# The first norm at row 8, the second convolution in pieces, projections from row 16, another place for the rows' store and the next x

## What is computed

```python
g = (mamba(x_n) + flip(mamba(flip(x_n)))) * scale_mod      # x_n = rmsnorm(x) * w
x = x + res_scale * (g + sigmoid(dwconv3x3(x_n) + b) * x_n)
# mamba: u, z = x_n @ W_in; u = silu(conv4(u) + b); dt, B, C = u @ W_x; delta = softplus(dt @ W_dt + b)
#        h[t] = exp(delta*A) * h[t-1] + delta*u*B;  y = sum_n C*h + u*D;  out = (y * silu(z)) @ W_out
t = t + attention(layernorm(t))      # 6 heads of 64, causal, softmax in f32
t = t + gelu(layernorm(t) @ w_fc.T) @ w_proj.T   # both weights are Kronecker products
```

## Time and profile before

| what | us |
|---|---|
| median of 3 runs (4754.21 to 4781.78) | 4765.77 |
| the profiled execution | 4750.03 |
| its span, first to last instruction | 4748.2 |
| busy: VectorE | 3668.8 (77%) |
| TensorE | 3452.2 (73%) |
| GpSimd | 2577.3 (54%) |
| ScalarE | 2460.6 (52%) |

### The profile page before, as it was taken

How to read it: one execution, slowest core, us unless ns; L and a number is a source line. 1 busy time by engine, 2 the same in 40 slices (tenths; PEclk the granted TensorE clock), 3 DMA queues, 4 the chain that set the end, 5 groups by cost and what they waited for, 6 DMA issues and landing times.

```text
span 4748.2 us, 40285 instructions
## 1 busy us (share of the span) xinstructions
PE 3452.2 (73%) x11626; PEld 1752.1 (37%) x11626; DVE 3668.8 (77%) x2793; ACT 2460.6 (52%) x3459; POOL 2577.3 (54%) x1628
## 2 busy tenths in 40 slices
PE   6300878778788778877688786877868776887897
PEld 2100325523364224632256232552336422462372
DVE  5899767889587987889868896888968798689221
ACT  3433446565364545645456454656546464565362
POOL 1789355565455565555656645656555557467100
PEclk9655889888798789988889888987889878997898
DMA  3999576787676786677957777778776778579200
GB/s 87 231 234 244 130 171 158 190 177 184 157 162 169 191 195 152 156 183 179 217 134 169 179 186 169 164 184 184 180 170 155 179 195 202 136 163 218 61 6 14
DMA packets 224022, 785.09 MB, mean 165 GB/s; under 512 B 25292, under 2 KB 40958, under 8 KB 223518
## 3 DMA queue, kind: packets, MB, share of 16 engines
q0 software_dynamic: 117504, 427.87, 47.1%
q1 hardware_dynamic: 106270, 354.32, 22.7%
HBM read 339.60 MB, written 39.85 MB: 80 GB/s over the span
## 4 chain that ended last, share of the span: by engine, by line
PE 40%; DVE 25%; issue 17%; ACT 7%; POOL 6%; DMA 5%; DVEq 0%; ACTq 0%; SPq 0%; POOLq 0%
DVE pBC L1146 15%; PE pW L638 8%; PE pW L560 8%; PE pW L451 7%; POOL hb L1322 5%; PE pW L615 3%; DMA y<-hb 2%; PE pW L493 2%; PE pW L471 2%; ACT pt L945 2%; DMA area<-in_x 2%; DVE hb L1114 2%; PE pW L576 2%; PE pW L527 2%; PE pW L695 1%
## 5 line engine op out<-in xcount | busy, mean ns | idle before, releaser
L1146 DVE TENSOR_TENSOR_SCAN pBC<-pBC,hb 128x1024 f32<-128x1024 f32 x768 | 1757.6, 2289 | 408.1 <-ACT pBC L785 235.9
L1336 POOL DMA_DIRECT2D y<-hb x792 | 763.6, 967 | 1005.2 <-DVE hb L1155 951.4
L1322 POOL TENSOR_TENSOR hb<-du_f,b_row 128x1024 f32<-128x1024 f32 x384 | 1018.5, 2661 | 148.2 <-DMA b_row<-bc_rows 93.4
L1322 POOL TENSOR_TENSOR hb<-uc_b,b_row 128x1024 f32<-128x1024 f32 x384 | 999.8, 2605 | 43.4 <-DMA y<-hb 42.1
L1155 DVE TENSOR_TENSOR hb<-pBC,c_row 128x1024 f32<-128x1024 f32 x768 | 940.5, 1225 | 46.4 <-DVE pBC L1146 2.7
L785 ACT ACTIVATE pBC<-delta,vec 128x1024 f32<-128x1024 f32 x384 | 429.9, 1119 | 424.4 <-DVE hb L1155 424.3
L785 ACT ACTIVATE pBC<-xres,vec 128x1024 f32<-128x1024 f32 x384 | 428.3, 1120 | 282.4 <-DVE hb L1155 281.7
L638 PE MATMUL pW<-area,pt 128*128 128x64 f32 x3456 | 459.2, 289 | 137.5 <-ACT pt L945 137.5
L1190 DVE TENSOR_REDUCE stat<-pW 128x1 f32<-128x640 f32 (+7 forms) x361 | 258.5, 753 | 317.5 <-PE pW L563 317.4
L638 PEld LDWEIGHTS pW<-area,pt 128*128 128x128 f32 x3456 | 429.8, 202 | 192.2 <-ACT pt L945 183.9
L471 PE MATMUL pW<-area,xn_area 128*128 128x512 f32 x576 | 290.3, 665 | 104.6 <-DVE xa L1138 52.2
(11 more groups left out here) (166 smaller groups left out, 4773.7 us busy)
## 6 DMA issues: line engine op xcount, KB each, us to landing
y<-hb POOLq DMA_DIRECT2D x792, 512.0 KB, 6.6
b_row<-bc_rows SPq DMA_DIRECT2D x256, 512.0 KB, 5.7
c_row<-bc_rows SPq DMA_DIRECT2D x256, 512.0 KB, 5.2
area<-in_x SPq DMA_DIRECT2D x8, 1536.0 KB, 16.2
kept_residual<-in_x SPq DMA_DIRECT2D x8, 1536.0 KB, 14.1
xres<-kept_residual SPq DMA_DIRECT2D x8, 1536.0 KB, 11.8
out_x<-xa SPq DMA_DIRECT2D x8, 1536.0 KB, 7.9
kept_residual<-hb POOLq DMA_DIRECT2D x16, 512.0 KB, 5.6
```

The costliest lines, as they stand in the source:

```text
L1146: dve.tensor_tensor_scan(flow(d, buf), flow(d, buf), flow(d, hb[slot(r)][:, :]), 0.0, ALU.mult, ALU.add).then_inc(scan_done, 1)
L1322: pool.tensor_tensor(hb[q % NHB][:, :], du[d][:, k, :], b_row[g % 2][:, :], ALU.mult)\
L1336: pool.dma_start(y[:, k, :], hb[q % NHB][:, :], accum_op=ALU.add).then_inc(y_in[k], 16)
```

## The change

The first norm moves to rows 8 to 15, in banks 0 and 1; the second convolution becomes six items (`conv`) in rows 9 to 18 in banks 2 and 3, each copied without Silu (`copy_u1`), with one Silu over each channel tile at row 21 (`step_silu`), the x projection at row 22 (`step_x`) and the narrow copies at row 24. RS goes from 18 to 27. The projections stand in rows 16 to 32, in the order q, v, k, and the groups of scores in rows 33 to 61 with row 47 free. The rows' store is taken at g = 9; w_v and w_k are loaded in the slots of proj 0 and 4. w_o goes into v_w, and q_pad changes sides. The next x is loaded into du_f in the slot of scores 16 (row 50), its squares go into area2. In sample 0 it is loaded at g = 18. Context lines are left out, and twelve columns of indent:

```diff
@@ -64 +64 @@
-RS = 18
+RS = 27
@@ -66,2 +66,4 @@
-         + [("step_u", 0, 10), ("step_u", 1, 14), ("step_bc", 0, 18)] + [("step_skip", k, RS - KT + k) for k in range(KT)]
-         + [(kind, k, 23 + 3 * k + i) for k in range(KT)
+         + [("conv", i, (9, 10, 12, 13, 17, 18)[i]) for i in range(6)]
+         + [("step_u", i, (11, 12, 15, 16, 19, 20)[i]) for i in range(6)]
+         + [("step_silu", 0, 21), ("step_x", 0, 22), ("step_bc", 0, 24)] + [("step_skip", k, RS - KT + k) for k in range(KT)]
+         + [(kind, k, 24 + 3 * k + i) for k in range(KT)
@@ -70 +72 @@
-Q0, S0, S1 = 24, 32, 63
+Q0, S0, S1 = 16, 33, 63
@@ -73 +75 @@
-def norm(n, r, gap):
+def norm(n, *rows):
@@ -75,2 +77 @@
-    return [("ln_mean", n, r)] + [
-        (kind, n, r + gap + i) for i, kind in enumerate(("ln_xc", "ln_var", "ln_rs", "ln_apply"))]
+    return list(zip(("ln_mean", "ln_xc", "ln_var", "ln_rs", "ln_apply"), [n] * 5, rows))
@@ -91 +92 @@
-    norm(0, 18, 2) + [("proj", t, Q0 + t * (S0 - Q0) // NPJ) for t in range(NPJ)] + attention()
+    norm(0, 8, 10, 11, 14, 15) + [("proj", t, Q0 + t * (S0 - Q0) // NPJ) for t in range(NPJ)] + attention()
@@ -95 +96 @@
-    + norm(1, S1 + 5, 2) + [("next_in", t, S1 + 7 + t // 2) for t in range(6)]
+    + norm(1, S1 + 5, S1 + 7, S1 + 8, S1 + 9, S1 + 10) + [("next_in", t, S1 + 7 + t // 2) for t in range(6)]
@@ -130 +131 @@
-        k_w, o_w = w_ko, w_ko
+        k_w, o_w = w_ko, v_w
@@ -177 +178 @@
-        xnext, xsq, rstd = tiled(area2), du_f, prob
+        xnext, xsq, rstd = du_f[:, :, :], tiled(area2), prob
@@ -187 +188 @@
-        q_pad = [t[:, :, :].rearrange("p k c -> p (k c)")[:, 0:L] for t in (w_ko, v_w)]
+        q_pad = [t[:, :, :].rearrange("p k c -> p (k c)")[:, 0:L] for t in (v_w, w_ko)]
@@ -353 +354,7 @@
-    if (kind, n) == ("proj", 5):
+    if (kind, n) == ("proj", 0) and not alone(b):
+        sp.wait_ge(cv_ready, at(12, b, 10))
+        load_weight(v_w, wv, v_in)
+    elif (kind, n) == ("proj", 4) and not alone(b):
+        sp.wait_ge(cv_ready, at(12, b, 12))
+        load_weight(k_w, wk, k_in)
+    elif (kind, n) == ("proj", 5):
@@ -363 +370 @@
-        load_weight(v_w, wv, v_in)
+        load_weight(k_w, wk, k_in)
@@ -370,2 +377,2 @@
-        load_weight(k_w, wk, k_in)
-    elif (kind, n) == ("ctx_t", 0) and more:
+        load_weight(v_w, wv, v_in)
+    elif (kind, n) == ("scores", 16) and more:
@@ -373 +380 @@
-        sp.wait_ge(pv_done, at(NG, a, NG))
+        sp.wait_ge(m1_done, at(ROWS, b, DROWS))
@@ -387,5 +393,0 @@
-        if more and not layer1:
-            sp.wait_ge(du_ready, at(6, b, 3))
-            sp.wait_ge(yd_ready, at(6, b, 3))
-            load_next(b + 1)
@@ -398 +400 @@
-            if g == 5:
+            if g == 9:
@@ -400,3 +402,3 @@
-                if layer1:
-                    load_weight(k_w, wk, k_in)
-                    load_weight(v_w, wv, v_in)
+            if g == NS + 2 and more and not layer1:
+                sp.wait_ge(m1_done, at(ROWS, b, DROWS))
+                load_next(b + 1)
@@ -476 +478 @@
-def causal(b, d):
+def causal(b, d, lo, hi):
@@ -479 +481 @@
-    for i in range(6):
+    for i in range(lo, hi):
@@ -481 +483 @@
-        if d == 0 and i < 4:
+        if d == 0:
@@ -484,5 +486,6 @@
-            pe.wait_ge(ip_evac, at(12, b, min(5 + i, 6)))
-        elif i < 4:
-            pe.wait_ge(ip_evac, at(12, b, 9 + i))
-        elif d == 0:
-            pe.wait_ge(uc_ready, at(6, b, i - 3))
+            if i < 4:
+                pe.wait_ge(ip_evac, at(12, b, min(5 + i, 6)))
+            else:
+                pe.wait_ge(uc_ready, at(6, b, i - 3))
+        elif i < 2:
+            pe.wait_ge(ip_evac, at(12, b, 11 + i))
@@ -490 +493 @@
-            pe.wait_ge(uc1_raw, at(2, b, i - 3))
+            pe.wait_ge(uc1_raw, at(6, b, i - 1))
@@ -493 +496 @@
-            mm = pe.matmul(pW[:, (i + 2 - 2 * d) % 4, :], cd[m][:, 128 * j:128 * j + 128],
+            mm = pe.matmul(pW[:, 2 + i % 2 if d else (i + 2) % 4, :], cd[m][:, 128 * j:128 * j + 128],
@@ -502 +505 @@
-        pe.wait_ge(uc1_ready, at(5, b, 5))
+        pe.wait_ge(uc1_ready, at(3, b, 3))
@@ -505 +508 @@
-            mm = pe.matmul(pW[0:56, c, :], xp_w[:, k, :], uc[d][:, k, c * HALF:(c + 1) * HALF],
+            mm = pe.matmul(pW[0:56, 2 * d + c, :], xp_w[:, k, :], uc[d][:, k, c * HALF:(c + 1) * HALF],
@@ -582 +585,5 @@
-    if kind == "step_in":
+    if kind == "conv":
+        causal(b, 1, n, n + 1)
+    elif kind == "step_x":
+        steps_in(b, 1)
+    elif kind == "step_in":
@@ -588,2 +595 @@
-                pe.wait_ge(xd_evac, at(4, latest(b), 4))
-                pe.wait_ge(uc1_ready, at(5, latest(b), 5))
+                pe.wait_ge(ip_evac, at(12, latest(b), 10))
@@ -601,2 +606,0 @@
-            pe.wait_ge(k_in, at(16, a, 16))
-        elif n == 12:
@@ -603,0 +608,2 @@
+        elif n == 14:
+            pe.wait_ge(k_in, at(16, a, 16))
@@ -608,3 +614,3 @@
-        if n < 12:
-            m, c = n % 6 // 2, n % 2
-            project(bank, (q_w, k_w)[n // 6], slice(128 * m, 128 * m + 128), xn1,
+        if n < 6 or n >= 14:
+            m, c = n % 14 // 2, n % 2
+            project(bank, (q_w, k_w)[n // 14], slice(128 * m, 128 * m + 128), xn1,
@@ -613 +619 @@
-            j = n - 12
+            j = n - 6
@@ -720 +726 @@
-        causal(b, 0)
+        causal(b, 0, 0, 6)
@@ -727,2 +732,0 @@
-        causal(b, 1)
-        steps_in(b, 1)
@@ -757,2 +761,3 @@
-    act.copy(dtr[d][0:RANK, :], pW[32:56, 0:2, :].rearrange("p b t -> p (b t)")).then_inc(xd_evac, 1)
-    act.copy(bc_raw[d], pW[0:32, 0:2, :].rearrange("p b t -> p (b t)")).then_inc(xd_evac, 1)
+    bank = pT if d else pS
+    act.copy(dtr[d][0:RANK, :], bank[32:56, :]).then_inc(xd_evac, 1)
+    act.copy(bc_raw[d], bank[0:32, :]).then_inc(xd_evac, 1)
@@ -800,0 +806 @@
+    m, c = i // 2, i % 2
@@ -802,2 +808,2 @@
-    act.activation(uc[1][:, 0, i * HALF:(i + 1) * HALF], pW[:, i % 4, :], ACT.Identity,
-                   bias=vec[:, 0, V_CB:V_CB + 1]).then_inc(uc1_raw, 1)
+    act.activation(uc[1][:, m, c * HALF:(c + 1) * HALF], pW[:, 2 + i % 2, :], ACT.Identity,
+                   bias=vec[:, m, V_CB:V_CB + 1]).then_inc(uc1_raw, 1)
@@ -807,7 +813,3 @@
-    act.wait_ge(uc1_raw, at(2, b, 2))
-    act.activation(uc[1][:, 0, :], uc[1][:, 0, :], ACT.Silu).then_inc(uc1_ready, 1)
-    for i in range(2, 6):
-        m, c = i // 2, i % 2
-        act.wait_ge(cv_ready, at(12, b, 7 + i))
-        act.activation(uc[1][:, m, c * HALF:(c + 1) * HALF], pW[:, i % 4, :], ACT.Silu,
-                       bias=vec[:, m, V_CB:V_CB + 1]).then_inc(uc1_ready, 1)
+    act.wait_ge(uc1_raw, at(6, b, 6))
+    for m in range(KT):
+        act.activation(uc[1][:, m, :], uc[1][:, m, :], ACT.Silu).then_inc(uc1_ready, 1)
@@ -842 +844 @@
-        act.wait_ge(uc1_ready, at(5, b, 5))
+        act.wait_ge(uc1_ready, at(3, b, 3))
@@ -880,6 +882,4 @@
-        if n == 0:
-            copy_u1(b, 0)
-            copy_u1(b, 1)
-        else:
-            silu_u1(b)
-            act.preload_act_table_set(LOG_EXP)
+        copy_u1(b, n)
+    elif kind == "step_silu" and not early:
+        silu_u1(b)
+        act.preload_act_table_set(LOG_EXP)
@@ -910,4 +909,0 @@
-        if n == 0:
-            act.wait_ge(bc_out[0], at(16, latest(b), 16))
-            act.wait_ge(bc_out[1], at(16, latest(b), 16))
@@ -930 +926 @@
-            ev = act.copy(vtok[:, n - 12, :], bank[:, 0:C])
+            ev = act.copy(vtok[:, n - 6, :], bank[:, 0:C])
@@ -932,0 +929,3 @@
+        if n == 0:
+            act.wait_ge(bc_out[0], at(16, latest(b), 16))
+            act.wait_ge(bc_out[1], at(16, latest(b), 16))
@@ -987 +986,2 @@
-        act.wait_ge(m1_done, at(ROWS, b, DROWS) if not isinstance(b, int) or b >= 0 else 0)
+        act.wait_ge(du_ready, at(6, b, 3) if not isinstance(b, int) or b >= 0 else 0)
+        act.wait_ge(pv_done, at(NG, b, 0))
@@ -1294 +1294 @@
-    if (kind, n) == ("proj", 14):
+    if (kind, n) == ("proj", 16):
@@ -1296 +1296 @@
-        pool.wait_ge(pj_ready, at(NPJ, a, 12))
+        pool.wait_ge(pj_ready, at(NPJ, a, 14))
```

More of the change, by code:

```diff
@@ L600, in item @@
                     elif n == 6:
+                        pe.wait_ge(v_in, at(16, a, 16))
+                    elif n == 14:
                         pe.wait_ge(k_in, at(16, a, 16))
-                    elif n == 12:
-                        pe.wait_ge(v_in, at(16, a, 16))
                     pe.wait_ge(ln_xn, at(4, a, 2))
```

## The result

The changed kernel takes 4592.92 us (median of 4 runs, 4585.77 to 4594.23) against 4760.43 us of the kernel before (4 runs): ratio 0.9637, 95% interval 0.9604 to 0.9671. Ratios are taken from the means of the runs without the profiler, one slow run each of `b_store7` and `a_all2` left out, so they are not exactly the quotients of the medians. I had forecast 4569 us within 4490 to 4690. The profiled execution has a span of 4589.8 us against 4748.2, so 158.4 us went; my sum had 196.7.

The account below looks back on a forecast made before the run. VectorE was taken to set the pace, so its idle time was priced: 4750.0 - 108.5 (to first scores) - 11.5 (sample 0) - 24.5 (attention) - 52.2 (next x) = 4553.3, plus 15.7 for the median: 4569 us, range 4490 to 4690.

Parts of the forecast that it names:

- The chain at row 18: SyncE's store order delays b_row, so VectorE waits 16.43 us at row 18; the wait goes with store at g = 9.
- Rows 16 to 19: Four projections, conv 4 and 5, copy and decay take 21.8 us against VectorE's 13.9: 7.9 us idle.
- The next x: Rows 67 to 73: earlier load lets the chain run 8.7 us earlier, -52.2 us over six samples.
- the lower clock at four places: Gaps before three step sizes and the x projection slow the work behind: 0 to 11.4 us a sample, 8 taken.
- row by row sum: Row 16 to the first scores: VectorE's stalls added row by row, 24.0 us idle a sample.
- the slower rival: Row 16 to scores: lower clock takes the whole stretch, idle 70 us a sample, 4833 us; chance 0.04.
- The free row: Attention rows: one free row instead of two, each costing 5.0 us less 1.4; -24.5 us over seven samples.
- sample 0: No projections: 14.6 + 1.3 us goes, 3.4 at row 27 and 1.0 at Silu come: -11.5 us.
- Rival 3: Projections lose as much as before, ScalarE behind TensorE in 17 rows: idle 45, 4660 us; chance 0.12.
- Rival 2: Row 18's wait moves to row 30's b_row or product 27, 12 us a sample: 4665 us; chance 0.10.
- rivals 1, 4 and 5: 1: lower clock throughout, 4833 us, 0.04; 4: next x gain hidden later, 4621, 0.10; 5: SyncE still held, 4766, 0.04.
- rival 6: Gaps stay without loss of clock and two free rows were worse than taken: about 4500 us; chance 0.10.

Follow-up runs that it names:

- b_store7: Kernel before with only the rows' store, and the w_k and w_v loads behind it, at g = 7 instead of g = 5: 4690.46 us, ratio 0.9838.
- a_all2: a_all with 8 more fillers ahead of the x projection and 10 ahead of next_in 0: 4431.84 us, ratio 0.9293.
- a_conv: Changed kernel with conv 4 and 5 in rows 14 and 15 and their copies in rows 13 to 16: 4535.52 us, ratio 0.9514.
- b_next: Kernel before with only the next x moved, into du_f in the slot of scores 16, squares in area2: 4701.18 us, ratio 0.9858.
- a_warm: Changed kernel with unused bf16 filler matmuls ahead of the three step sizes (8, 16, 16) and scores 0 (16): 4505.53 us, ratio 0.9459.
- b_three: b_both with the scores in rows 32 to 59 without a free row between them: 4593.66 us, ratio 0.9617.
- b_both: Kernel before with the store at g = 7 and the next x moved, nothing else: 4640.91 us, ratio 0.9720.
- a_store8: Changed kernel with the rows' store at g = 8 instead of 9: 4593.38 us, ratio 0.9642.
- a_all: Changed kernel with conv 4 and 5 in rows 14 and 15, the fillers of a_warm and no free attention row: 4443.41 us, ratio 0.9325.

## Why the prediction was right, and where it was off

**Right.** The chain at row 18 was read rightly: SyncE's store ahead of b_row. `b_store7` moves it, with the weight loads behind it, and the wait falls to what the accumulate leaves. Rows 16 to 19: 7.9 forecast, 7.4 measured, and `a_conv` shows the term to be TensorE's work. Rows 27 and 28 behind the skip terms: 3.4 forecast, 3.3 measured. The next x: -52.2 forecast, -54.2 measured, and -50.9 where `b_next` moves it alone; rsqrt now follows the last wo projection and the mean. The waits worked out by adding durations along a named chain came out within 1 us, those behind a gap of TensorE once the gap was filled: 1.1, 1.0, 0.6 and 4.2 with fillers for 1.3, 1.0, 0.6 and 4.5, and row 24 with the fillers of `a_all2` at 2.3 for 2.3. The range was 200 us wide, so that the time fell into it says less than these terms do.

**Mis-sized: the clock.** The sum took 24.0 us of idle a sample to the first scores at full clock, and 8 more for the lower clock at four places (the three step sizes at 3.2 each and the x projection at 1.7), with 11.4 as the upper bound. Measured are 252.7 / 7 = 36.1, so 12.1 on top of the 24.0, beyond the bound. In sample 3 the four places cost all that they could: rows 26, 29 and 32 waited 2.8, 2.4 and 4.5 us longer than the row by row sum had, 9.7 together for 9.6, and row 24 1.7 for 1.7. I had taken 8 of the 11.4 although, as the prediction itself says, nearly every such gap of the kernel before had cost its price. A fifth place that I had not counted is the scores before row 33, 5.35 us for 4.5. The groups behind them run slowly too: the second and third lost 1.2 and 1.4 us a sample in the changed kernel, and 0.1 and 0.8 with fillers. With the fillers of `a_warm`, which leave the x projection as it was, the idle is (593.87 - 416.94) / 7 = 25.3: the row by row sum stands, and 10.8 of the 12.1 is the clock at the three step sizes and the scores. The 4.1 us beyond my 8 are 29 of the 38 us that the sum missed, over seven samples.

The rule of the Trainium skill that was weighed there ("TensorE: Matmul & The Clock Gate", section "HAM oscillation — how this bites in real kernels") did bite: the bursts behind the waits of 2.2 to 4.6 us in sample 3 began below full clock, with 10.86 us for three projections against 7.99. It did not take the whole stretch, as the slower rival had it: 10.86 is well under twice 7.99, so the full clock came back inside the burst, and the granted clock to the first scores was 0.82 to 0.84.

**The free row: nearly right.** -24.5 forecast, -16.7 measured. The wait at row 49 is 4.8 us a sample, near its price of 5.0, and `b_three` against `b_both` gives 3.6 a free row for the 3.5 taken. 6 of the 8 us between are in the second and third group: together they lose 2.6 us a sample in the changed kernel and 1.8 in the profile before (from 0.8 to 2.5 there, by the sample). That is the clock again, since with fillers ahead of the scores they lose 0.9. But `b_both`, with the old places, also loses 2.4 there, and against it the attention rows gained 22.6. So part of the shortfall is how the one profile before fell out.

**Missed: sample 0.** -11.5 forecast, -5.5 measured. Rows 1 to 33 lost 10.2 us of idle, near the forecast. But the next x, loaded at row 48 beside rows that run at 3.46 us, took 18.0 us to land, and the b_row behind it was late: VectorE waited 3.19 us at row 57. `b_next` and `b_both`, which move the load and leave the other places, have the same wait (3.02 and 2.93). I had named the delay, with a bound of 8 us, and taken 0.

```profile
332.92 2.30 DVE L1146 TENSOR_TENSOR_SCAN pBC<-pBC,hb 128x1024 f32<-128x1024 f32 x1 [3.19 <-POOL hb L1322]
```

```profile
330.48 2.33 POOL L1322 TENSOR_TENSOR hb<-uc_b,b_row 128x1024 f32<-128x1024 f32 x1 [3.86 <-DMA b_row<-bc_rows]
```

**The rivals.** Rival 3 (the projections lose as much as before) has a true core: in absolute terms the idle fell, but after the store is out of the way the new places give only about 28 us. What 20 projections in eight rows lost came back as 7 us of convolution in the way (`a_conv`), gaps that cost clock (`a_warm`), and Silu with more behind it (rows 23 and 24, which no run took away). Rival 2 (row 18's wait moves) did not happen, and `a_store8` shows that there is slack left. Nothing was seen of rivals 1, 4 and 5: the granted clock was 0.82 or more over the stretch to the first scores in every sample, `b_next` has the gain of the next x, and the parts came by stage. Of rival 6 the opposite held, since the gaps did lose clock.

## What to carry to other kernels

Read a large, regular wait back through every in-order queue before rebuilding a schedule: here one number in the issuing engine's order and one buffer gave a ratio of 0.972, where a rewrite of the whole plan gave 0.964. When work is spread thinner to fit beside the bounding engine, price TensorE's gaps as well as its work, since the burst behind a gap can run slower, and a wait that is put down to ScalarE can be TensorE's. Where a gap can't be filled with work, throw-away matmuls into a bank that is about to be overwritten are worth a try: 56 of them a sample took 4593 us to 4506 here (0.9637 to 0.9459). Their number is tuned to one schedule: in `a_all` the same fillers miss a gap in four samples of seven.

## What the runs showed of the hardware that was not expected

Short gaps were enough here: TensorE was idle 2.6, 4.6 and 3.7 us before the three step sizes, and each time the work behind ran below full clock, 2.96 to 3.78 us for a step size that takes 1.98 with fillers, at a granted clock of 0.75 over the stretch. The idle time just before does not settle it alone: the same 2.18 us ahead of the x projection went with 7.05 us of work in six samples of the changed kernel and with 5.36 in the first. And the fillers needn't be the kernel's own type: with bf16 matmuls ahead of it, the f32 work of the same stretch had a granted clock of 0.97. Engines beside it saw no cost that could be read in the trace; VectorE's busy time in that stretch is the same 39.74 us.
